# First attention: units of two batches and half of their queries, with joined near products

## The reference, cut to what matters

```python
buckets = _relative_position_bucket(N, N)          # 40 buckets, by key - query
pos_bias = jnp.transpose(rel_embed[buckets], (2, 0, 1))
...
gate_out = gate_a * (gate_b * gru_const - 1.0) + 2.0   # by batch, head and query
gated_bias = gate_out * pos_bias[None]
scores = jnp.einsum('bhid,bhjd->bhij', q, k) * scale + gated_bias
attn = jax.nn.softmax(scores, axis=-1)
out = jnp.einsum('bhij,bhjd->bhid', attn, v)
```

## Time and profile before

| | |
|---|---|
| median of 3 runs | 2298.37 us (2298.21 to 2301.98) |
| the profiled execution's own time | 2297.82 us |
| its span | 2296.0 us |
| PE, DVE, ACT, POOL busy, share of the span | 87%, 71%, 59%, 48% |
| the first attention's products | from 124.8 to about 1011 us of the span |

### The profile page before, as it was taken

How to read it: one execution, slowest core, us unless ns; L and a number is a source line. 1 busy time by engine, 2 the same in 40 slices (tenths; PEclk the granted TensorE clock), 3 DMA queues, 4 the chain that set the end, 5 groups by cost and what they waited for, 6 DMA issues and landing times. The chain is left out here.

```text
span 2296.0 us, 56479 instructions
## 1 busy us (share of the span) xinstructions
PE 2004.4 (87%) x17787; PEld 1018.4 (44%) x17787; DVE 1625.2 (71%) x3441; ACT 1348.2 (59%) x2150; POOL 1099.2 (48%) x987
## 2 busy tenths in 40 slices
PE   5569999999999999975799759999999999998576
PEld 3324444444444444444344214444444444444355
DVE  4778888888888888767565776666666666664696
ACT  2226666666666666542455437777777777777121
POOL 1132322232223222414355317877877787877464
PEclk8869999999999999986899979999999999999787
DMA  5521111122112211100000460011111011100000
GB/s 133 156 62 51 55 54 49 50 55 53 49 50 55 53 49 51 47 11 1 1 1 0 154 194 29 29 41 28 41 28 42 28 42 28 42 14 1 0 14 23
DMA packets 127050, 107.03 MB, mean 47 GB/s; under 512 B 39636, under 2 KB 102724, under 8 KB 126956
## 3 DMA queue, kind: packets, MB, share of 16 engines
q1 hardware_dynamic: 124640, 103.37, 16.5%
q10 hardware_dynamic: 2316, 2.64, 0.4%
HBM read 76.01 MB, written 29.53 MB: 46 GB/s over the span
## 5 line engine op out<-in xcount | busy, mean ns | idle before, releaser
L1048 DVE TENSOR_REDUCE b_mx<-psum 128x1 f32<-128x512 f32 x1024 | 663.8, 686 | 145.7 <-PE psum L867 82.6
L1032 ACT ACTIVATE b_prob<-psum 128x1024 f32<-128x1024 f32 x512 | 524.3, 1024 | 319.8 <-PE psum L899 319.7
L1806 POOL TENSOR_TENSOR f_plo<-f_prob,f_phi 128x512 f16<-128x512 f32 x512 | 587.6, 1158 | 169.4 <-ACT f_phi L1931 144.2
L1949 DVE TENSOR_REDUCE f_mx<-psum 128x1 f32<-128x512 f32 x512 | 328.7, 683 | 169.0 <-PE psum L1826 167.9
L1930 ACT ACTIVATE f_prob<-psum 128x512 f32<-128x512 f32 x512 | 308.1, 602 | 158.1 <-PE psum L1837 153.4
L947 PE MATMUL psum<-b_prob,b_v 128*32 128x256 f32 x4096 | 328.3, 392 | 1.6 <-ACT b_prob L1032 0.5
L1931 ACT ACTIVATE f_phi<-psum 128x512 f16<-128x512 f32 x512 | 306.4, 598 | 0.0
L805 POOL COPY b_v<-v 128x64 f32 x64 | 15.2, 238 | 596.1 <-PE psum L947 595.8
L899 PE MATMUL psum<-b_diag,b_toep 128*128 128x79 f16 (+1 forms) x4224 | 267.4, 208 | 0.0
L899 PEld LDWEIGHTS psum<-b_diag,b_toep 128*128 128x128 f16 x4224 | 235.9, 99 | 9.1 <-issue 2.6
L808 POOL TENSOR_TENSOR b_diag<-flip,grev 128x1024 f16<-128x1024 f16 x128 | 239.8, 1895 | 0.0
(11 more groups left out here) (312 smaller groups left out, 3407.4 us busy)
## 6 DMA issues: line engine op xcount, KB each, us to landing
d_qk<-e_qk SPq DMA_DIRECT2D x64, 256.0 KB, 2.6
b_toep<-d_line SPq DMA_DIRECT2D x128, 64.0 KB
f_qa<-d_qk SPq DMA_DIRECT2D x64, 128.0 KB, 2.8
f_ka<-d_qk SPq DMA_DIRECT2D x64, 128.0 KB, 2.9
b_q<-d_q SPq DMA_DIRECT2D x128, 54.0 KB
d_k<-a_qk SPq DMA_DIRECT2D x48, 128.0 KB, 2.3
b_toep<-d_line SPq DMA_DIRECT2D x128, 32.0 KB
b_q<-b_m SPq DMA_DIRECT2D x256, 1.0 KB
```

The source lines that it names most:

```text
L1032: nc.scalar.activation(prob[:, t % 4, :].rearrange("p (a n) -> p a n", a=2), ps[:, EXP + 2 * (t % 2):EXP + 2 * (t % 2) + 2, :], ACT.Exp).t ...
L1048: nc.vector.tensor_reduce(mx[:, b, t, half:half + 1], ps[:, bank, :], AX.X, ALU.max).then_inc(s.max_read, 1)
L1806: nc.gpsimd.tensor_tensor(plo[:, t % 4, at], prob[:, t % 4, at], phi[:, t % 4, at], ALU.subtract).then_inc(s.plo_ready, 1)
L1949: nc.vector.tensor_reduce(mx[:, b, t, half:half + 1], ps[:, MAX + half, :], AX.X, ALU.max).then_inc(s.max_read, 1)
```

## The change

A unit is now a head, a pair of batches and half of their queries: idx 0 and 1 are the pair (0, 1), idx 2 and 3 the pair (2, 3), and idx % 2 (called hf) chooses query quarters hf and 2 + hf of each of the two batches. There are still 64 units of 8 steps. In a step, key tile t stands against 2 x 512 queries: bank i holds quarter 2i + hf of both batches, 256 columns each. The near products of exp take both batches in one matmul, 2 x 128 or 2 x 79 columns, since the Toeplitz matrix is the same. Query tiles belong to one of two units, so a step has six near products, three or none. The far products of exp have 256 columns or fewer and are issued for the first batch of the pair, then come those of the maxima, then exp's for the second batch. Each exp bank has its own semaphore.

The diagonals lie in memory that other stages use (`combT`, `x16`), apart for maxima and exp; GpSimd forms three per head and batch where it formed two. Loads are apart too: `load_max` (14 DMAs for a pair) and `load_exp` (16). The Toeplitz matrices are loaded once for a pair for exp, and only the high part for the maxima. `store_m` issues eight DMAs of two rows per unit instead of four of four rows. OUT_STEP goes from 2 to 3: "o" is turned behind step 3 and divided at step 4. `divide_o` multiplies in two instructions, one for each batch. ORDER (natural) and LAG = 1 (values one step behind) are new names for what the kernel did. At the stage's start GpSimd clears 21 semaphores of the stage before.

```diff
@@ constants
+        LAG = 1
+        QUARTER = N // 4
+        ORDER = ((0, 1, 2, 3, 4, 5, 6, 7), (0, 1, 2, 3, 4, 5, 6, 7))
...
-        OUT_STEP, M_STEP = 2, 4
+        OUT_STEP, M_STEP = 3, 4
...
+        MAX_LOADS, EXP_LOADS, M_STORES = (8, 6), 16, 8
+
+        def query_tile(idx, n):
+
+            bb, i, y = n // 4, n // 2 % 2, n % 2
+            return 2 * (idx // 2) + bb, 4 * i + 2 * (idx % 2) + y
@@ sync
-                    for half in range(2):
-                        for part in range(2):
-                            row, at = half * GROUP + M_ROW + part, (2 * half + part) * (TB // 2)
-                            sp.dma_start(qs[b][row:row + 1, half * BANK:(half + 1) * BANK].rearrange("a (t p) -> a t p", p=P),
-                                         m16[at:at + TB // 2, b % 2, :]).then_inc(m_stored[b], 16)
+                    for bb in range(2):
+                        for i in range(2):
+                            for part in range(2):
+                                row, at = i * GROUP + M_ROW + part, 8 * bb + 4 * part + 2 * i
+                                q0 = i * BANK + (idx % 2) * QUARTER
+                                sp.dma_start(qs[2 * (idx // 2) + bb][row:row + 1, q0:q0 + QUARTER].rearrange("a (t p) -> a t p", p=P),
+                                             m16[at:at + 2, idx % 2, :]).then_inc(m_stored[idx], 16)
...
+                sp.wait_ge(s.zeroed, 2)
+                load_max(0, 0)
+                load_exp(0, 0)
+                sp.wait_ge(s.zeroed, SLOTS)
+                load_max(0, 1)
                 store_m(0, 0)
                 with sp.Fori(0, H0 - 1) as k:
-                    for b in range(B):
-                        store_m(k + (b + 1) // 4, (b + 1) % 4)
-                        load(k + 1, b)
...
+                    load_exp(k, 1)
+                    store_m(k, 1)
+                    load_max(k + 1, 0)
+                    store_m(k, 2)
+                    load_exp(k + 1, 0)
+                    store_m(k, 3)
+                    load_max(k + 1, 1)
+                    store_m(k + 1, 0)
@@ gpsimd
+                def for_max(h, pair):
+                    for half in range(2):
+                        pool.wait_ge(s.max_psum[half], done(TB * (4 * (h - 1) + 2 * pair + 1) + TB - 1))
+                    for b in (2 * pair, 2 * pair + 1):
+                        nc.gpsimd.tensor_tensor(diag_max[:, b, :, :], flips, gates(h, b, 0), ALU.mult).then_inc(s.diag_max_ready, 1)
+
+                def for_exp(h, pair):
+                    pool.wait_ge(s.av_ready, done(TB * (4 * (h - 1) + 2 * pair + 1) + TB - 1))
+                    for b in (2 * pair, 2 * pair + 1):
+                        nc.gpsimd.tensor_copy(vs[:, b, :, 0:D0], g.v[:, b * TB:(b + 1) * TB, bass.ds(h * D0, D0)])
+                        for part in range(2):
+                            ins = nc.gpsimd.tensor_tensor(diag_exp[:, b, part, :, :], flips, gates(h, b, part), ALU.mult)
+                    ins.then_inc(s.v_diag_ready, 1)
@@ tensor
-                    return [x for x in near if half * BANK <= x[1] * P < (half + 1) * BANK]
+                    return [x for x in near if x[1] // 2 == 2 * i + hf]
...
-                            last = nc.tensor.matmul(ps[:, bank, at + x:at + y], toep[:, b, tp, blk * P:(blk + 1) * P], diag[:, b, dp, qt, x:y],
+                            last = nc.tensor.matmul(both[:, :, at + x:at + y], toep_exp[:, pair, tp, blk * P:(blk + 1) * P],
+                                                    diag_exp[:, 2 * pair:2 * pair + 2, dp, qt, x:y],
                                                     start=False, stop=(tp, dp) == (1, 0), skip_group_check=True)
...
+                def both_scores(h, idx, pos, ahead):
+
+                    wait_exp(h, idx, pos)
...
                     for left in (False, True):
+                        for i in range(2):
+                            last[i] = exp_far(0, i, idx, pos, left) or last[i]
+                    if ahead:
+                        at = [ring.index((pos, half)) for half in range(2)]
                         for half in range(2):
-                            last = exp_far(b, t, half, left) or last
+                            bank_free(h, idx, at[half])
+                        fars = max_fars(im, nm, [RING + x % BANKS for x in at])
+                    for left in (False, True):
+                        for i in range(2):
+                            last[i] = exp_far(1, i, idx, pos, left) or last[i]
                     if ahead:
...
+                        max_nears(im, nm, [RING + x % BANKS for x in at], fars)
+                    for i in range(2):
+                        (exp_near(i, idx, pos) or last[i]).then_inc(s.exp_psum[i], 1)
@@ vector
-                    nc.vector.tensor_tensor(out, o[:, :, :, 0:D0], rl[:, b % 2, :, :].rearrange("p x (c a) -> p x c a", a=1).to_broadcast([P, 2, 4, D0]),
-                                            ALU.mult).then_inc(s.o_ready, 1)
...
+                    for bb in range(2):
...
+                        ins = nc.vector.tensor_tensor(out, o[:, :, :, bb, 0:D0], r[:, :, :, bb:bb + 1].to_broadcast([P, 2, 2, D0]), ALU.mult)
+                    ins.then_inc(s.o_ready, 1)
```

More of the change, by code:

```diff
@@ L704, in phase_attend0 @@
         s.max_read = sem("b_max_read")
-        s.exp_psum = sem("b_exp_psum")
+        s.exp_psum = [sem(f"b_exp_psum{i}") for i in range(2)]
         s.exp_ready = sem("b_exp_ready")
@@ new lines, in load_exp @@
+                def load_exp(h, pair):
+                    for i in range(2):
+                        sp.wait_ge(s.exp_psum[i], done(TB * (4 * (h - 1) + 2 * pair + 1) + TB - 1))
+                    head = bass.ds(h, 1)
+                    j = exp_loaded[pair]
+                    for bb in range(2):
+                        b = 2 * pair + bb
+                        for half in range(2):
+                            mine, tok = slice(half * BANK, (half + 1) * BANK), bass.ds(b * N, N)
+                            part = bass.ds(b * N + half * BANK, BANK)
+                            rows = slice(half * GROUP, half * GROUP + M_ROW)
+                            sp.dma_start(qs[b][rows, mine], one(g.d_q[head, :, part])).then_inc(j, 16)
+                            for side in range(2):
+                                sp.dma_start(ks[b][side][rows, :], one(g.d_k[side, head, :, tok])).then_inc(j, 16)
@@ L774, in _ @@
-                for b in range(B):
-                    sp.sem_inc(m_stored[b], 64)
-                    sp.wait_ge(s.zeroed, b + 1)
-                    load(0, b)
+                    for bb in range(2):
+                        for i in range(2):
[4 more added lines that the diff above has]
+                                             m16[at:at + 2, idx % 2, :]).then_inc(m_stored[idx], 16)
@@ L886, in exp_far @@
                         return
-                    rows = slice(half * GROUP, (half + 1) * GROUP)
-                    both = c0 < mid < c1
-                    return nc.tensor.matmul(ps[:, bank, x - c0:y - c0], ks[b][int(not left)][rows, t * P:(t + 1) * P], qs[b][rows, x:y],
-                                            start=not (left and both), stop=not exp_near_of(t, half), skip_group_check=True)
-                def exp_near(b, t, half):
-                    bank, c0 = EXP + 2 * (t % 2) + half, half * BANK
+                    rows = slice(i * GROUP, (i + 1) * GROUP)
@@ new lines, in exp_far, with exp_near @@
+                    opens = bb == 0 and not (left and c0 < mid < c1)
+                    at = bb * QUARTER - c0
+                    return nc.tensor.matmul(ps[:, bank, at + x:at + y], ks[b][int(not left)][rows, t * P:(t + 1) * P], qs[b][rows, x:y],
+                                            start=opens, stop=not exp_near_of(t, i, hf), skip_group_check=True)
+                def exp_near(i, idx, pos):
+                    pair, hf = idx // 2, idx % 2
+                    t, bank = ORDER[hf][pos], EXP + 2 * (pos % 2) + i
+                    both = ps[:, bank, :].rearrange("p (b q) -> p b q", b=2)
@@ L915, in maxima, with max_fars, max_nears @@
+                def max_fars(idx, n, banks):
+                    b, t = query_tile(idx, n)
+                    return [max_far(b, t, half, banks[half], right) for right in (False, True) for half in range(2)]
+                def max_nears(idx, n, banks, fars):
+                    b, t = query_tile(idx, n)
                     for half in range(2):
@@ L935, in both_scores @@
-                    for half in range(2):
-                        last = exp_near(b, t, half) or last
-                    last.then_inc(s.exp_psum, 1)
-                def values(h, b, t):
-                    item = 4 * h + b
-                    tile = TB * item + t
-                    if t == 0:
+                            bank_free(h, idx, at[half])
[3 more added lines that the diff above has]
+                            last[i] = exp_far(1, i, idx, pos, left) or last[i]
@@ L944, in values @@
```

(11 more changed lines are left out.)

165 lines of the change are left out of this document (89 added, 76 removed).

## The result

The changed kernel takes **2501.05 us** (median of 4 runs, 2495.62 to 2501.24), the kernel before 2300.18 beside it: a ratio of 1.084, 95% interval 1.0763 to 1.0917 (the medians give 1.087; one of the four runs before took 2325.6). Medians are over all runs, ratios leave out slow ones, over 1.5% above the fastest of their kernel. Slower, as forecast, but by 200 us instead of 75, outside the range. The profiled span is 2499.2, 203 more than before. The first attention ends its last copy of m at 1190.2 us; in the kernel before it did at 997.3, so 193 of the loss lie in this stage. The other 10 stay unexplained.

A forecast was written before the change was run, and what follows sets the result against it. The prediction took TensorE's own work to set about 12.3 of 13.5 us an item, VectorE the rest. Late stores of m add 1.25 us over 60 units, 75 us: 2297.8 + 75 = 2373 us, range 2290 to 2430.

The forecast's parts named there:

- Its sum: Chain from T0 to T0: 9.1 to m's copy, 0.02 to first issue, 3.99 to last, 1.64 to release: 14.75 us.
- T0: Start of a unit's first step; the forecast counts the way to m's copy and its stores from there.
- stores late at full clock: Main case: TensorE waits 1.1 us for m at each unit, clock stays full; 2373 us, chance 0.55.
- Near products joined: TensorE's near products of exp: 66 become 33 an item, columns are the price; saving taken as 0.
- Far products: TensorE's far products of exp: 22 per batch become 36; cost taken as 0, upper bound 0.4 us per unit.
- OUT_STEP: Values turned a step later: division and turning of m some 0.4 to 0.7 us later, copy ends at T0 + 9.1.
- first kind: Unit with tiles 0, 1, 4, 5 as queries; the second kind has 2, 3, 6, 7. Copy forecast T0 + 9.1 or 8.9.
- Stores: Stores of m on SP: eight issues 0.57 us apart, 3.99 from first to last, then 1.64 to the release.
- Edits that cost nothing: GpSimd's third multiplication, some 2 us more per item, fewer loads, ScalarE's second wait and semaphore clearing: no cost in the loop.
- The clock: Rival: TensorE's waits drop its clock to half; 20 units falling add 60 us, 2433; chance 0.11.
- stores hidden: Rival: eight small stores issue in 0.37 us each, m lands before TensorE is ready; 2307 us, chance 0.22.
- a fixed price of a product: Rival: each near product costs 0.052 us whatever its width, joining saves 1.7 us a unit; 2250 us, chance 0.09.

The follow-up runs named there:

- both repairs: Changed kernel with GpSimd's second-batch work held until VectorE has joined the maxima, and four four-row stores of m a unit instead of eight: 2308.33 us, ratio 1.0023.
- The pair of runs on the kernel before: Kernel before, GpSimd's work of an item moved by one wait: onto VectorE's joining of the maxima 2590.24 us; behind it, as control, 2300.68 us.
- Both runs that fill the wait: 20 unread 256-column products put in TensorE's 2.86 us wait: in the changed kernel 2540.69 us; in the changed kernel with four-row stores 2383.95 us.
- merged stores: Changed kernel with m's high and low rows side by side, so four stores of four rows replace eight of two: 2430.81 us, ratio 1.053.
- mending the lock alone: Changed kernel, but GpSimd waits between the two batches of its exp diagonals until VectorE has joined the maxima: 2447.24 us, ratio 1.0599.

## Why the prediction was wrong

Its sum was 14.75 a unit. Measured in the windows' two units: from T0 to the end of m's copy 9.37 and 11.72 (509.60 - 500.23, 527.39 - 515.67), to the last issue 4.28 and 4.38, to the release 1.79 and 1.88. Together 15.44 and 17.98, mean 16.71. Against 13.5 that is 3.2 x 60 = 193 of the 200 us. The forecast's own range for stores late at full clock had a slip: its terms, 25 more and 18 either way, give 2355 to 2416 around 2373, not 2345 to 2400.

*Near products joined, 0:* right. 0.63 and 0.30 as forecast, and 0.64 apart. It left out that 132 products and as many weight loads fewer in a pass of the loop also shorten the code, here worth 101 us (2409.23 - 2308.33): not a gain over the kernel before, but a loss averted.

*Far products, 0:* right; with both repairs the pair takes 27.2 with them.

*OUT_STEP:* the number was right by luck, the mechanism wrong. Without the lock a unit of the first kind reaches its copy's end at T0 + 8.9 (526.27 to 535.17 in the kernel with both repairs) and one of the second kind at 9.0 or 9.4; mean 9.0, against 9.1 in the forecast, which had the first kind later. But the later turning isn't what moved it from 8.81: the edit alone took the kernel before from 8.81 to 8.74, and taking it back in the kernel with both repairs gave 9.1 for 9.0. Where the 0.2 come from stays open. In time the edit gains 5 to 10 us where the stores have slack, which I didn't consider.

*Stores:* the mechanism was right, the size too small. 0.61 apart, not 0.57, and 1.8 to the release, not 1.64: 6.16 instead of 5.65, 0.5 a unit, 31 us. The range held that.

*"Edits that cost nothing":* **the step that failed.** It let GpSimd's third multiplication go because "each result has over half a unit to spare", asking only who waits for GpSimd's results. The cost is in whom its instructions block while they run. They were bunched for two batches, 11.5 us without a gap, and so lay on the join once a pair: 11.72 instead of 8.9, 1.4 a unit on average, 84 us. The kernel before had a sign of it, which I missed by not looking at the longest of a group (timelines of VectorE and of GpSimd):

```profile
964.61 3.16 DVE L1058 CAST b_mm<-b_negm 128x8 f16<-128x8 f32 x1
963.84 3.92 POOL L814 CAST w<-wT 128x4480 f16<-128x4480 f32 x1
```

GpSimd's instruction ends at 967.76, the conversion at 967.77. This is the very wait, 2.75 us, that the forecast took from the earlier trace rows for what a fall of the clock costs, without asking why VectorE was late. With the stores' 31 this makes 115 of the 118 between 75 and 193. The pair of runs on the kernel before (290 us for moving GpSimd's work, some 30 of them stops at the jump) shows it as a cause.

Behind this stands a rule of the Trainium skill, "SBUF — State Buffer", section "Who interferes with whom": VectorE in a two-port mode, or with two inputs in SBUF, and a GpSimd instruction share one pair of ports as an exclusive lock, and the second waits for the whole of the first. The subtraction (two inputs in SBUF) waited, the PSUM readings and the reduction with its one input didn't: the trace agrees. The conversion (one input) waited too, which fits the rule if it ran in a two-port mode; no run here shows its mode.

*The clock:* it fell in 31 stretches, where I gave that rival 0.11 and priced it as an addition. Both runs that fill the wait say it must be placed. In the changed kernel the fall lies between the copy of m and the next unit, under the stores, and filling its wait only moved it to a place where it cost 40 us. It counts where nothing else is waited for: 47 us with merged stores. So the two repairs don't add up: mending the lock alone leaves waits for m of 1.8, whose falls slow the way to the next copy (T0 + 10.35 or 11.8 behind a fall, 9.2 to 9.4 without); mending the stores alone bares the fall behind the join.

*Rivals:* stores hidden, no, they came 0.61 apart with a wait behind them; a fixed price of a product, no, by the blocks of 0.63 and 0.64.

## What to carry to other kernels

Before calling work on GpSimd free, lay its instructions over VectorE's and ask which SBUF-to-SBUF conversions and two-input instructions fall under them, however small: an eight-element conversion waited about 1 us, and moving the work 4.5 us later cost 290, while 2 us more gave them back. Look at the longest of a group, not its median, and price a fall of the clock where it lies, on the path or under another wait. Where the unrolled loop is long, watch the instruction queue: a small edit can cost a fetch at each jump.

## What was unexpected of the hardware

TensorE's granted clock fell to half (1.2 GHz) behind single idle stretches, but not behind all. In the loops of all runs here, counting those that began at full clock:

| idle time of TensorE | stretches | clock fell behind |
|---|---|---|
| 1.1 to 1.7 us | 193 | 0 |
| 1.8 to 1.9 us | 56 | 41 |
| 2.0 to 4.8 us | 180 | 179 |

With the 2.86 filled to 0.70 it stayed at full.

Fetching code at a loop's jump cost 2.8 to 4.8 us and, with the fall behind it, 4.5 to 7 a unit: at 1478 and 1558 instructions of TensorE in a pass never seen, at 1742 at each jump, at 1615 to 1629 in some kernels at none, in others at some or all. Probably that also widens the runs of such kernels (2283 to 2322 with OUT_STEP 3); only one run of each has a profile.
